# A decoder of four layers on one core: a new interleaving of three groups' steps, and new bank pairs

## The reference

```python
x = _layernorm(x + _L0_attn_ref(x, ...))            # "rec"
x = _layernorm(x + _L0_xattn_ref(ctx_1024, x, ...)) # "x0", 16 heads
x = _layernorm(x + _L0_ffn_ref(x, ...))             # "f0", 8 experts
...                                                 # a1 x1 f1, a2 x2 f2, a3 x3
x = _layernorm(x + _L3_ffn_ref(x, ...))             # "f3": conv, attention, 8 gated experts
return x
```

## Time and profile before

| what | before |
| --- | --- |
| median of three runs | 5807.09 us (5786.76 to 5812.85) |
| the profiled execution | 5791.86 us, span 5790.1 us |
| TensorE busy | 5007.7 us, 86% |
| VectorE busy | 3545.7 us, 61% |
| ScalarE busy | 2402.6 us, 41% |
| GpSimd busy | 711.2 us, 12% |
| mean granted TensorE clock | 0.926 of full |

### The profile page before, as it was taken

The page is one execution under the profiler, slowest core; times in us unless marked ns, Lnnn a source line. Parts: engine busy times, 40 slices in busy tenths (PEclk is TensorE's granted clock), DMA queues, the critical chain, the costliest instruction groups (busy, mean ns, idle before and its releaser), DMA issues.

```text
span 5790.1 us, 132736 instructions
## 1 busy us (share of the span) xinstructions
PE 5007.7 (86%) x56369; PEld 3671.1 (63%) x56369; DVE 3545.7 (61%) x9529; ACT 2402.6 (41%) x4619; POOL 711.2 (12%) x735
## 2 busy tenths in 40 slices
PE   5765888899998989998889999889998988989887
PEld 3544666666766666766666667666676756666564
DVE  7572576755666665567566566656657565756552
ACT  3111444544434444444444444444444344443431
POOL 6361000101000010100010010001100010100010
PEclk7576889999998999999899999998999989999997
DMA  1113000011110001210100111010110100100000
GB/s 58 25 41 100 30 12 20 2 39 56 42 39 7 25 10 35 63 40 30 31 2 25 35 48 47 23 31 10 30 54 15 54 15 31 35 27 25 9 30 26
DMA packets 144939, 184.72 MB, mean 32 GB/s; under 512 B 46074, under 2 KB 73826, under 8 KB 143714
## 3 DMA queue, kind: packets, MB, share of 16 engines
q1 hardware_dynamic: 144354, 176.23, 10.2%
HBM read 164.32 MB, written 11.57 MB: 30 GB/s over the span
## 4 chain that ended last, share of the span: by engine, by line
PE 70%; DVE 11%; ACT 7%; issue 2%; DMA 1%; POOL 0%; SPq 0%; POOLq 0%; DVEq 0%; ACTq 0%
PE g_bank L2646 8%; PE g_bank L2661 8%; PE g_bank L1552 6%; PE g_bank L1574 6%; PE g_bank L1524 6%; ACT g_keys_exps L1604 3%; DVE g_tops L1617 3%; PE g_bank L1585 3%; PE g_bank L1494 2%; PE g_bank L2385 2%; PE g_bank L1909 2%; PE g_bank L1433 2%; PE g_bank L1899 2%; PE g_bank L1388 1%; PE g_bank L1992 1%
## 5 line engine op out<-in xcount | busy, mean ns | idle before, releaser
L1604 ACT ACTIVATE g_keys_exps<-g_bank 77x512 f32<-77x512 f32 (+1 forms) x1536 | 802.7, 596 | 632.9 <-PE g_bank L1552 632.2
L1617 DVE TENSOR_REDUCE g_tops<-g_bank 128x4 f32<-128x308 f32 (+1 forms) x1536 | 813.9, 575 | 367.3 <-PE g_bank L1524 364.8
L1367 POOL TENSOR_TENSOR g_rstd<-g_rstd,minus_half 128x4 f32<-128x4 f32 x224 | 228.2, 1020 | 4275.1 <-DVE g_rstd L1349 4274.8
L2661 PEld LDWEIGHTS g_bank<-region,g_keys_exps 128*128 128x128 f32 x4096 | 517.8, 192 | 169.6 <-issue 152.9
L2646 PE MATMUL g_bank<-g_xT,region 128*128 128x512 f32 x1024 | 555.2, 624 | 22.1 <-DVE g_keys_exps L2686 10.3
L2661 PE MATMUL g_bank<-region,g_keys_exps 128*128 128x128 f32 x4096 | 546.5, 278 | 11.1 <-DVE g_base L2693 10.0
L1552 PE MATMUL g_bank<-g_qa,g_keys_exps 32*77 32x128 f32 (+1 forms) x12288 | 474.3, 294 | 60.9 <-DVE g_o L1637 36.1
L1552 PEld LDWEIGHTS g_bank<-g_qa,g_keys_exps 32*77 32x77 f32 (+1 forms) x12288 | 396.9, 177 | 175.5 <-DVE g_o L1637 60.3
L1598 ACT ACTIVATE g_oT_sc<-g_bank 128x512 f32<-128x512 f32 x384 | 229.9, 599 | 615.9 <-PE g_bank L1574 615.6
L1574 PE MATMUL g_bank<-g_keys_exps,g_v 77*32 77x128 f32 (+1 forms) x12288 | 438.0, 286 | 53.7 <-DVE g_tops L1617 48.6
L1524 PE MATMUL g_bank<-g_keys_exps,g_qa 32*128 32x154 f32 (+1 forms) x6144 | 400.7, 373 | 91.8 <-ACT g_keys_exps L1604 75.1
(11 more groups left out here) (377 smaller groups left out, 8974.8 us busy)
## 6 DMA issues: line engine op xcount, KB each, us to landing
region<-L_w_in SPq DMA_DIRECT2D x512, 256.0 KB, 2.8
region<-xT_in SPq DMA_DIRECT2D x16, 256.0 KB, 2.6
z_scratch<-m_uT SPq DMA_DIRECT2D x1, 4096.0 KB, 11.0
g_oT_sc<-z_scratch SPq DMA_DIRECT2D x16, 256.0 KB, 2.9
g_xT<-xT_in SPq DMA_DIRECT2D x16, 256.0 KB, 3.7
g_o<-x_in SPq DMA_DIRECT2D x16, 256.0 KB, 4.1
out<-g_x SPq DMA_DIRECT2D x16, 256.0 KB, 2.3
region<-weights_in SPq DMA_DIRECT2D x1, 3020.5 KB, 10.6
```

Of the source, the lines that this page charges most:

```text
L1367: e.tensor_tensor(g.rstd[:, :], g.rstd[:, :], g.s["minus_half"], ALU.pow).then_inc(*b.gpsimd(st + " rstd"))
L1604: e.activation(g.p[0:nk, r, :, :], bank[r][0:nk, :].rearrange("p (u q) -> p u q", u=4), ACT.Exp, scale=scale).then_inc(*b.scalar(f"{st} p ...
L1617: e.tensor_reduce(g.tops[:, :, first:first + 2], src, AX, ALU.max).then_inc(*b.vector(f"{st} top {n} {r}"))
L2661: ins = e.matmul(bank[1][:, n * D:(n + 1) * D], g.gated_hid[:, x % 2, c, n * T:(n + 1) * T], weights.part(f"w2 {x}", c), start=c == n == 0 ...
```

## The change

`ORDER` and `GIVEN` hold other digits. Nothing else differs: no instruction, buffer, wait of a group on itself, generator or size. By the words that describe the change, the strings come from a search outside the kernel, which lays the steps out one after another by assumed durations; in the new one ScalarE's and VectorE's durations are those of the trace, and ten unfinished orders are carried side by side. All strings have the same length as before, and each engine's digits occur as often.

```diff
 ORDER = {
     "tensor": (
-        "0000000000000000000000000000000000000000000000000000000000010111110000001100110100110010011010010110"
-        "1010010110101001101010100010101001010111110101100110111111010101211021012002202211111121122121122101"
...
+        "0000000000000000000000000000000000000000000000000000000000000000010100101110010101100101100101010100"
+        "1010110100010111001010110011000001000101000011011010110111111111101110011101010022002222121111121210"
+        "2211122101202112212122120002001120221212121021212020111010202021011000220222022020020222222202021022"
...
     "scalar": (
-        "0000000000000000000000000000000000000000000000001001010011011100111100111110101111010111110000100011"
...
+        "0000000000000000000000000000000000000000000000000000001010111111001111010111101011110000100111011010"
...
     "vector": (
-        "0000000000000000000000000000000000000000000000000000000000000000000000000000000100000000001000111111"
...
+        "0000000000000000000000000000000000000000000000000000000000000000000000000000000000000000000000100010"
...
     "sync": (
-        "000000111111222222bbaaaabbaaaaaaaaaaaaaaaaaaaaaaaaaaaaaaaaaaaaaaaaaaaaaaaabbbbbbbbbbbbbbbb0000000bbb"
-        "bbbbbbbbbbbbbaaaaaa1111111aaaaaaaaaaaaaaaaaaaaaaaaaabbbbbbbbbbbbbbbb2222222aaaaaaaaaaaaaaaabbbbbbbbb"
...
+        "000000111111222222babaaabbaaaaaaaaaaaaaaaaaaaaaaaaaaaaaaaaaaaaaaaaaaaaaaaabbbbbbbbbbbbbbbb0000000bbb"
+        "bbbbbbbbbbbbaabaaaaaaaaaaaa1111111aabbbbbbbbbbbbbaabbaabaaaaaaaaaaaa2222222aaaaaaaaaaaaaaaabbbbbbbbb"
...
 GIVEN = (
-    "00010203101201130003112221132200131200012203110011122003130211002100231200021311220011222311132220030311"
...
+    "00010203001211130200130120221320010012231001230012232001121023011002132221031003012220111300221311231220"
...
+    "0011132022031122101122230111002302211200112300110203202302010223200322010221000302030001")
```

More of the change, by code:

```diff
@@ new lines @@
+        "2122102021101010021212211221221221112121201220120220220200220220201101201122012000211202100222120200"
+        "1212020022210120112011222020201201012001011011112122122221220110010001001001112010101021120010110010"
+        "0110100010111010202201220111201211020120120120202212112021012001001021222112121021201012202022020202"
+        "0020022020200020212201102101101211221212121021021121021001011012022012110002100200120101021002100010"
+        "1210020100120102120020000100100101000100102010220001200201221220021000110100010011121212111221221111"
@@ new lines @@
+        "2100202200201210202201021121021201202110210101011101011010110112201120210011201110011021012011211221"
+        "1011011011212111210111021211100112110022002111100200200220020000200202021021212101200200201001110010"
+        "1221012022001210122012022100221222012122210202210201110222201200220012010212012212202202222021221020"
+        "2102220221002021201212210112212000210221202011011111111111112202002221211111212122110120001210012121"
+        "2211210121221102110212112212010020121120012210101011010010111010001011101001012012002000000012012101"
@@ new lines @@
+        "0221102202020221122102000222202222120120001020201010110121212221021200210112120201101120210102101120"
+        "2010212012121121220100100200100102121201100110010101110010011101010100210210012022020201011100202101"
+        "2121201010100102101120220022002022022020210201110111011001010010100101212212202021221101001001021100"
+        "1000010010210210010100021122020022010201002100210020020020120120012211001012002000200202002002000210"
+        "0221122002012012211212211121221211121222112010120102220002102100210211201021010110110211221102110021"
@@ new lines @@
+        "0121121201211020020112101112121121110101101110110211221211212210220111211021121211012011110022000202"
+        "2000220020001100100200202120110212221212122010001001002201020121010101101201200121121020212012100112"
+        "1002020022012100200212221121212211211220110210211121111001121120110120220200202122101201100221201120"
+        "2201102212222212111221222221012002210202012210202012122112122211102122211120120122122221221102100201"
+        "0211122012011011010101010220200022202020022010110121010121120002221200022221212022220022121120102110"
@@ new lines @@
+        "0101010001101001001010211020102111112021002221220111022122221211222120222020122012010111020202102211"
+        "2121221211201002020100221020101221012220022022101102102102200201101102101201021011020020200021212112"
+        "1011211202102021222211212120121010010101001010111010100212202120022102210110002010101201200011211022"
+        "0221012002102020002000000202020002000222002000200022200200201200012001000100011020010000010010010100"
+        "1020010011122122111211222120210201012121220012100102022211211102121021101211021110010111102102100210"
@@ new lines @@
+        "2112102101020121021100121021021021112121011011011111101102121200012210202022010021002000020020000020"
+        "2221121020201200112010020010112220020201202112002100102121001001120122010201001001101010121012102020"
+        "2221010000100100101101110210112121111111120110112210021002022022021211221121021121211202011112120001"
+        "0210202112012201201222012212212200201220222000221022120212122122212202200220220201222012122212212212"
+        "0222122021210102201021201111010110100022020002220201200112021011101210202002212220121220020021221021"
```

346 lines of the change are left out of this document (157 added, 189 removed).

## The result

| | before | after |
| --- | --- | --- |
| median of 20 runs each | 5804.56 us | 5826.82 us |
| lowest to highest | 5786.76 to 5815.99 | 5809.96 to 5849.52 |
| ratio | | 1.004 [1.003, 1.0049] |
| the profiled execution | 5791.86 us | 5821.41 us |

The forecast of 5765.1, which meant faster by 0.7%, was wrong in sign and 61.7 us too low, though the range, which reached to 5840, held the time. By its mechanism only (a) fits, as shown further down.

A forecast was written before the change was run, and what follows sets the result against it. The prediction took TensorE, with some 650 short holes behind VectorE and ScalarE, as the bound. Terms -35 - 10 + 1 + 2 = -42 us gave 5749.9 profiled, 5765.1 as median; range 5740 to 5785, reaching to 5840 with rivals.

The forecast's parts named there:

- (a): Rival: nothing moves, TensorE's holes that go are replaced by others of the same size; +9 us, 5816; chance 0.30.
- What bounds the kernel: TensorE, with some 650 short holes where VectorE's or ScalarE's result comes late; idle 584.8 us from 500 us on.
- (b): Rival: VectorE's in-order queue holds ready steps, delaying TensorE; +50 us, 5857, or smaller form +27, 5834; chance 0.15.
- The holes behind VectorE and ScalarE, -35: TensorE's 538.9 us of waits shrink by the shortfalls' ratio 0.935, -35 us; bounds -54 to +6.
- The second count, +6: TensorE waits with under 8 matmuls of cover, counted without durations and priced by source line; sum +6 us.
- TensorE's busy time at equal clock must be as before: Sign in the profile after: at equal clock, TensorE's busy time is unchanged.
- The clock, -10: Less idle time on TensorE raises its clock; -10 us, bounds 0 and -39.
- Start and end, +1: Third group starts after 1004 matmuls instead of 932, +2.5 us; ends of groups 1 and 2, -2.0 and +0.4; together +1.
- loads, +2: Loads used under 20 matmuls after release rise from 42 to 66; TensorE's DMA waits +2 us, bounds 0 and +11.
- The banks, 0: TensorE's waits for another group's last read of its pair, 19 to 32 with little cover; 0 us, bound +11.
- the prediction is wrong if the waits stay at 540 us: Sign that would refute the forecast: TensorE's waits on VectorE and ScalarE, 538.9 us before, don't fall.
- The sign named for a wrong direction: Wrong in sign if VectorE's waits on TensorE fall while TensorE's on VectorE rise.

The follow-up runs named there:

- second profiles: One more profiled run of each order: banks_before for before's; for after's, the changed kernel unaltered, 5815.94 us, ratio 1.0032 to the kernel before.
- start_after: After's order up to TensorE's step 1740, then before's, pairs of banks renamed to fit; 5810.17 us, ratio 1.0016 to the kernel before.
- banks_before: Kernel before, same order of steps, its pairs of banks dealt by another rule (373 of 608 digits stay); 5804.95 us, ratio 1.0003.
- same_switches: Kernel before with 73 of TensorE's steps moved by one or two places, changes of tile shape kept at 1874; 5827.03 us, ratio 1.0041.
- start_before: Before's order up to TensorE's step 1740, then after's, pairs of banks renamed to fit; 5808.37 us, ratio 1.0012 to the kernel before.

## Why the prediction was wrong

*What bounds the kernel* stands. TensorE with its short holes is still the bound, and VectorE's waits on TensorE became longer (VectorE's waits from 500 us on, first of kernel before, then of kernel after):

```profile
DVE g_tops L1617 <- PE g_bank L1524: 354.6, 265, 6.6
DVE g_keys_exps L2686 <- PE g_bank L2646: 245.1, 167, 6.0
```

```profile
DVE g_tops L1617 <- PE g_bank L1524: 382.7, 272, 6.5
DVE g_keys_exps L2686 <- PE g_bank L2646: 275.5, 177, 5.2
```

Rival (b), by which VectorE would have held TensorE back more, is ruled out: VectorE's part of TensorE's waits fell by 2.6 us, where (b) wanted over 8% more. That its smaller form lies only 7 us from the time is luck.

*The holes behind VectorE and ScalarE, -35.* This is the step that failed. The waits fell by 538.9 - 529.0 = 9.9 us, DMA took 6.3 of them back, and all idle time fell by 3 us (583 to 580, and 581 to 577 in the second profiles of each order). The count of shortfalls was right on its own ground: it said fewer long ones, and holes over 1.5 us lost 16.3 us. It was wrong to apply its ratio to all 538.9 us. Two thirds of that idle time sat in holes under 1.5 us (389.0 of 577.5 us), and these grew by 12.7 us, to 401.7. The shortfalls were a demand that nothing carries from wait to wait; a ratio of such demands is no ratio of idle times.

*The second count, +6.* Its size was nearer, its lines were not. L1552 was to rise by 15 us and went from 59.2 to 59.4; L1524 with 88 tight places instead of 89 rose by 7.9; L1537, which that count didn't list, fell by 11.0; L1585 fell by 7.2 where 1.9 stood, L1547 by 6.1 where 2.2 stood. L1574 fell by 3.5 where 3.0 stood, the one term that came out. The two largest rises were on lines that it didn't price, L1388 by 11.6 (all its rows, 20.2 to 31.8) and L1999 by 9.4. A sum near the truth came from terms that missed.

*A term that the prediction did not have: TensorE's own time, +17.* It was assumed that "TensorE's busy time at equal clock must be as before". By the table it went from 4496 to 4513 us (4492 to 4516 in the second profiles). Of this 12 to 13 lie in the middle and 5 in the end. The prices of a change and of a hole, in the last section, can't simply be multiplied by the 42 changes and 30 holes that the middle has more, because at a boundary that has both they don't add up, and because a part of each is paid inside the next step. So I added the time beyond the usual for every boundary and every step of the traces at full clock, scaled to all steps. In the middle the boundaries come to 175 us in after and 167 in before, the steps themselves to 5 us more; in the end it is 3 and 3 us more, in the start 1 and 1. The second profiles of both orders give the same within 3 us. All together that is 21 us against 17 to 24 by the table, and covers both the middle and the end.

*The clock, -10.* There was nothing to win, since the idle time stayed: this term fell with the one above it. The rule of the Trainium skill that the prediction weighed (TensorE: Matmul & The Clock Gate, "A second HAM failure mode: psum-queue depth-cycling") was not put to the test, as there was no such fall in micro-idles. By the table slow clock excess is 228 and 253 us with before's order, 244 and 232 with after's: the same within what one order shows twice. Inside that, the start is 24 us worse and the end about 17 better. The timed start_after puts the start's whole loss at 9 us (2 to 16), so the three profiles overstate it.

*Start and end, +1; loads, +2.* The third group's later entry was priced by idle time alone, and the start's idle time is unchanged (220 and 221). The loss there is at the clock, some 230 us and more after the beginning of the phase. The end gained 12 us by time (4 to 19), where -1.6 stood. The waits for loads rose by 6.3 us, within 0 to +11, and 4.8 of that at L1677 (14.5 to 19.3), where the prediction had all of it at the weights. The loads' order alone was not tried.

*The banks, 0* fits, as far as banks_before tests it; after's own pairs can't be tried on before's order.

*The sum as it came out.* In the profiles: own time +17, idle time -3, slow clock excess +16, together +30 us (the phase is 31 longer, before rounding), of which some 7 are the fast profile of before. Over both profiles of each order the clock's +16 goes to -2, and own time's +20 and idle time's -3 make +15. In the medians: +22 us. By parts and timed: start +9, middle +21, end -12, together +18. The middle's timed 21 us (13 to 31) is more than the 12 that its own time shows; what stands behind the rest stays open.

*Where the profile speaks.* Of the signs named beforehand, "the prediction is wrong if the waits stay at 540 us" came true, at 529 us. So did the failure of "TensorE's busy time at equal clock must be as before". VectorE's share stayed at 330.8 us where 305 was said, and L1388 rose where it was to fall. The number of waits over 1.5 us did fall, and L2661 and L2646 with it. The sign named for a wrong direction, VectorE's waits on TensorE falling while TensorE's on VectorE rise, did not appear, and the direction was wrong all the same: only the sign of busy time at equal clock watched what TensorE does where it doesn't wait. TensorE's idle time in the first 100 us of the phase (31.8 us, 31.5 before) and the mean clock of 0.95 were as said, and prove nothing.

## What to carry to other kernels

Here an order laid out by durations shortened the long waits and not the sum of all: take a gain only from the holes that a count can see, one by one, and expect small ones to come back. Ask also what a boundary between two steps costs where nothing waits, since a new order changes the boundaries too. Where two orders agree in every group's count at some step, cut there and time the pieces; one piece of a losing order may win, and here it was the end. Where one chain runs alone on TensorE, a few matmuls that nobody reads can raise its clock and pay: 0.34% here with both fillings in before's order, and nothing measurable in after's.

## What the runs showed of the hardware

*A change of tile shape on TensorE costs some 0.1 us between the steps, and up to as much again inside the next full-array step.* From the start of a step's last matmul to that of the next step's first one, at full clock and without idle time (medians over all sixteen traces): behind L2661 112 ns to a full-array step (6093 places) and 205 to one of 32 rows or columns (1378); behind L1585 109 and 202; behind L2646 429 and 522. Behind L1552 it is 89 to another step of 32 rows and 200 to the rest. Then, from the first to the last matmul of the next step: L2661 takes 779 ns behind a full-array step and 883 behind another shape, L2646 433 and 534, the transposes of L1585 327 and 383. The Trainium skill (TensorE: Matmul & The Clock Gate, "The mechanism" in "Packing small matmuls — row/col tiling") says that a weight load overlaps a matmul in flight only where the row group differs. The trace doesn't bear that out as the cause: steps of the full array and of 32 columns both take all rows, and still it is 205 ns from one to the other, 112 between two of the first (L2661) and 89 between two of the second (L1574). The cause stays open.

*A hole costs more than the idle time that the profile gives it.* Less the idle time shown, the same stretch between two steps is 163 ns longer with a hole than without where the shape stays (275 against 112 behind L2661), and 70 where it changes (275 against 205). So a change of shape costs nothing between the steps where there is a hole anyway. Inside the next step a hole adds 75 ns to L2661 (854 against 779) and 72 to L2646 (505 against 433). same_switches, with 32 more holes and no more changes, has 6 us more own time, 0.19 us each. The Trainium skill (TensorE: Matmul & The Clock Gate, "Single matmul latency") has the drain of a bf16 matmul at roughly 175 ns beside the columns; the trace's 163 agrees in size, though these are f32 and no run shows that it is the drain. So the idle time in a trace of TensorE understates what its stalls cost.

*The clock differs between executions of one order.* before and banks_before, the same order, have 228 and 253 us of slow clock excess and phases 20 us apart; start_before has 112 us of it in a middle where after has 89. A difference of 20 us between two single profiles of this kernel is no finding.

*Matmuls that nobody reads raise it.* 0.61 to 0.87 and 0.62 to 0.96 in the filled stretches, for 0.2% and a further 0.14%, of which the second is within the intervals of the two runs. The chain beside it was not held up: in the same 94 us VectorE does 80 instructions in both kernels, and TensorE its own 473 and, of 731, some 483 besides the 248 of the filling.
